# Moving two pairs of squares and a table preload to a later place in ScalarE's order

## The chip, the cores and the metric

The kernel runs on all 8 cores of one Trainium2 chip. Each core works on its own two of the sixteen sequences with no exchange between cores, and the metric is the device time in microseconds of the slowest core. A core has a matrix engine (TensorE, PE in the profile), a vector engine (VectorE, DVE), an engine for activation functions (ScalarE, ACT), GpSimd (POOL) and SyncE (SP). Each runs its own instruction stream in order, and semaphores order the streams against each other. Of POOL and SP only the DMA queues matter here: SP loads x, POOL stores the result.

## The reference

It is one adaLN layer over x of 16 sequences x 4096 tokens x 1024 channels, in float32. The modulation rows come from a small product; then there are two residual branches.

```python
mod = (silu(c) @ wmod).reshape(16, 6, 1, 1024)
sa, ca, ga, sb, cb, gb = mod[:, 0], ..., mod[:, 5]
h = layernorm(x) * (1 + ca) + sa
h = h @ w_in.T + b_in
state = sigmoid(a) * state + b * h_t        # scan over the 4096 tokens' order
x = x + ga * (ys @ w_out.T + b_out)
h = layernorm(x) * (1 + cb) + sb
x = x + gb * tanh(h @ weight @ aux_weight1 @ aux_weight2 + bias)
```

The attention stand-in is a linear input projection, a first-order scan along time, and a linear output projection. The feed-forward branch is three linear maps in a row, which the kernel multiplies together once into a single matrix Wc, and a tanh.

## The kernel before, in words

A setup part builds the combined matrix, the modulation vectors and the broadcast rows (about the first 475 us). The main part then walks over 8192 tokens per core in 32 chunks of 256 tokens (two blocks `tb` of 128). Every float32 matrix product is made as three bf16 products of high and low halves, which DVE splits off (`v_split`).

The main part is one loop over 33 periods, `k` = 0 to 32, on every engine. A period holds the scan branch of chunk k, the second half (LN2, feed-forward) of chunk k-1, and the first layer norm (LN1) of chunk k+1. The order of each stream is written out by hand in `stream_T` (TensorE), `stream_V` (VectorE) and `stream_SC` (ScalarE):

- TensorE: MM1(k), 8 groups i = 0 to 7 of 24 matmuls (`t_MM1`, L702), each group into PSUM bank 2 + i % 2; then the transposes TR2(k-1) and TR1(k+1) (L682); then MM3(k-1) (L750) and MM2(k) (L725). Group i of MM1 waits until ScalarE has taken group i-2 out of its bank (`prev23`).
- ScalarE: evU(k, i) copies group i of MM1 out of PSUM with scale and bias into `su` (L808). SQ(k+1, 1) and SQ(k-1, 2) (`sc_SQ`, L766) are two Square instructions each, over 128x1024, whose accumulated sums are the second moments for LN1 and LN2; they write the squares themselves into `sLNxm1`, which is scratch then. SQRT (L778) makes the standard deviation out of the variance that DVE returns. evA and ev2 (L785, L795) take out the transposes, TANH (L818) ends the feed-forward branch.
- VectorE: v_epiA (residual of branch one, L636 to L646), scans of groups 0 and 1 (`v_scan`, L619), v_LN2 (L578 to L599), scans 2 and 3, v_LN1 (L547 to L568), scans 4 to 7, three splits, and v_epiF (L659 to L671).

Both layer norms bounce between the two engines. DVE reduces x to a sum (L578 in LN2), waits for ScalarE's squares ("sq2"), computes the variance (L582 to L588, "vv2"); ScalarE takes the root ("sqrt2"); DVE goes on with the reciprocal and normalises. The tanh and the square root need different activation tables, so each period changes the table twice. L913 is a Sqrt on one column into a dummy tile, `s_dum`: it has the table for Sqrt loaded ahead of the first real SQRT. In period 32 there is no chunk k, so no evU; in periods 31 and 32 there is no SQ(k+1, 1).

SP loads chunk k+1 of x into one of three buffers `sx` once the store of chunk k-2 is out ("xload", "store").

Of the kernel before, what the change touches and what calls it, by code (L numbers as in the profile page):

```python
# [9 lines left out]
AF = mybir.ActivationFunctionType  # L10
# [8 lines left out]
NCH = TC // CH  # L19
# [5 lines left out]
def build_program(tc=TC, debug=False):  # L25
    EMIT_LOG.clear()
    NCH = tc // CH
# [24 lines left out]
    with contextlib.ExitStack() as stp:  # L52
        def sb(name, shape, dt=F32):
            return stp.enter_context(nc.sbuf_tensor(name, shape, dt))
# [17 lines left out]
        s_A = sb("s_A", [128, KB])  # L72
# [406 lines left out]
        s_dum = sb("s_dum", [128, 1])  # L479
# [40 lines left out]
        E = EV()  # L520
# [239 lines left out]
        def sc_SQ(E, sc, k, which):  # L760
            xap = lambda tb: sx[:, k % 3, tb, :]
            acc = s_s2a if which == 1 else s_s2b
            for tb in range(TB):
                if tb:
                    E.op(lambda: sc.drain())
                f = (lambda tb=tb: sc.activation(  # L766
                    sLNxm1[:, 0:4, :], xap(tb), AF.Square,
                    accum_out=acc[:, tb:tb + 1]))
                if tb < TB - 1:
                    E.op(f)  # L770
                else:
                    E.inc(s_sq, f, ("sq1" if which == 1 else "sq2", k))

        def sc_SQRT(E, sc, k, which):
            vin = s_vara if which == 1 else s_varb
            vout = s_sda if which == 1 else s_sdb
            E.wait(("vv1" if which == 1 else "vv2", k))
            E.inc(s_sq, lambda: sc.activation(vout[:], vin[:], AF.Sqrt),  # L778
                  ("sqrt1" if which == 1 else "sqrt2", k))

        def sc_evA(E, sc, k):
            bi = k // NBCH
            for j in range(KB):
                E.wait(("tr1", k, j))
                E.inc(s_b01, lambda j=j, bi=bi: sc.activation(  # L785
                    sLNxm1[:, j, :], pb[j % 2][:, 0:CH], AF.Identity,
                    scale=s_ca1[:, bi * 8 + j:bi * 8 + j + 1],
                    bias=s_sa[:, bi * 8 + j:bi * 8 + j + 1]),
                    ("evA", k, j))

        def sc_ev2(E, sc, k):
            bi = k // NBCH
            for j in range(KB):
                E.wait(("tr2", k, j))
                E.inc(s_b01, lambda j=j, bi=bi: sc.activation(  # L795
                    sLNxm2[:, j, :], pb[j % 2][:, 0:CH], AF.Identity,
                    scale=s_cb1[:, bi * 8 + j:bi * 8 + j + 1],
                    bias=s_sb[:, bi * 8 + j:bi * 8 + j + 1]),
                    ("ev2", k, j))

        def sc_evU(E, sc, k, i0=0, i1=KB):
            for i in range(i0, i1):
                E.wait(("mm1", k, i))
                if i >= 2:
                    E.wait(("scan", k, i - 2))
                elif k >= 1:
                    E.wait(("scan", k - 1, i + 6))
                E.inc(s_b23, lambda i=i: sc.activation(  # L808
                    su[:, i % 2, :], pb[2 + (i % 2)][:, 0:CH], AF.Identity,
                    scale=s_bv[:, i:i + 1], bias=s_bbi[:, i:i + 1]),  # L810
                    ("evU", k, i))

        def sc_TANH(E, sc, k):
            for tb in range(TB):
                E.wait(("epiFp", k, tb))
                if tb:
                    E.op(lambda: sc.drain())
                E.inc(s_th, lambda tb=tb: sc.activation(  # L818
                    sy_flat[:, tb * D:(tb + 1) * D],
                    sy_flat[:, tb * D:(tb + 1) * D], AF.Tanh),  # L820
                      ("tanh", k, tb))
# [78 lines left out]
        def stream_SC(E, sc):  # L900
            E.eng, E.engname = sc, "scalar"
            E.wait(("xload", 0))
            sc_SQ(E, sc, 0, 1)
            sc_SQRT(E, sc, 0, 1)
            sc_evA(E, sc, 0)
            for k in range(NPER):
                if k + 1 < NCH:
                    E.wait(("xload", k + 1))
                    E.wait(("vv1", k))
                    E.wait(("spA", k))  # L910
                    sc_SQ(E, sc, k + 1, 1)
                E.op(lambda: sc.drain())
                E.op(lambda: sc.activation(s_dum[:], s_A[:, 0:1], AF.Sqrt))  # L913
                if k < NCH:
                    sc_evU(E, sc, k, 0, 2)
                if 0 <= k - 1:
                    E.wait(("x2", k - 1))
                    E.wait(("vv2", k - 2) if k >= 2 else None)
                    sc_SQ(E, sc, k - 1, 2)
                if 0 <= k - 1:  # L920
                    sc_SQRT(E, sc, k - 1, 2)
                if k < NCH:
                    sc_evU(E, sc, k, 2, 4)
                if k + 1 < NCH:
                    sc_SQRT(E, sc, k + 1, 1)
                if k < NCH:
                    sc_evU(E, sc, k, 4, KB)
                if 0 <= k - 1:
                    if k < NCH:
                        E.wait(("spA", k))  # L930
                    sc_ev2(E, sc, k - 1)
                if k + 1 < NCH:
                    sc_evA(E, sc, k + 1)
                if 0 <= k - 1:
                    sc_TANH(E, sc, k - 1)
# [4 lines left out]
        stream_T(E, None)  # L940
        stream_V(E, None)
        stream_SC(E, None)

        E.plan = False
        EMIT_LOG.append(("__BLOCK__", "bar", "", 0))
        with nc.Block() as blk:
            @blk.sync
            def _(sy):
                stream_sync(E, sy)

            @blk.gpsimd
            def _(gp):
                stream_gp(E, gp)

            @blk.tensor
            def _(te):
                stream_T(E, te)

            @blk.vector
            def _(ve):  # L960
                stream_V(E, ve)

            @blk.scalar
            def _(sc):
                stream_SC(E, sc)
# [68 lines left out]
```

How the kernel before makes its waits and increments, by code:

```python
        def W(eng, engname, smp, val):  # L110
            EMIT_LOG.append((engname, "w", NAME[id(smp)], val))
            if val > 0:
                eng.wait_ge(smp, val)
# [1 line left out]
        def I(ins, engname, smp, val=1):  # L115
            EMIT_LOG.append((engname, "i", NAME[id(smp)], val))
            return ins.then_inc(smp, val)
# [383 lines left out]
            def inc(self, sem, f, key=None, by=1):  # L501
                nm = NAME[id(sem)]
                if self.plan:
                    v = self.counts.get(nm, 0) + by
                    self.counts[nm] = v
                    if key is not None:
                        assert key not in self.events, key
                        self.events[key] = (sem, v)
                else:
                    EMIT_LOG.append((self.engname, "i", nm, by))
                    f().then_inc(sem, by)
# [1 line left out]
            def wait(self, key):  # L513
                if key is None or self.plan:
                    return
                sem, v = self.events[key]
                EMIT_LOG.append((self.engname, "w", NAME[id(sem)], v))
                self.eng.wait_ge(sem, v)
```

## Time and profile before

| | |
|---|---|
| median of 12 runs | 2985.88 us (2972.57 to 3238.04) |
| the profiled execution's own time | 2979.61 us |
| its span on the slowest core | 2977.9 us |
| spans of the 8 cores | 2957.1 to 2977.9 us |
| busy in the span | PE 86%, DVE 49%, ACT 24%, POOL 1% |
| mean granted TensorE clock | 0.927 of full speed |

The span runs from the first to the last instruction of the slowest core; the execution's own time is 1.7 us longer. In the timelines below, a row gives the start in us, the duration in us, the engine, the line, the operation, what is written and read, how many instructions are merged into the row, and in brackets the idle time of the engine just before it, with what ended that idle time. A PE row's end is modelled, and consecutive PE rows overlap.

### The profile page before, as it was taken

The page shows a single profiled execution, that of the slowest core. Times are in us where ns is not written, and L with a number is a line of the kernel's source. Part 1 is how long each engine was busy: PE and PEld are TensorE (multiplying, and loading weights), DVE is VectorE, ACT ScalarE, POOL GpSimd, SP SyncE. Part 2 cuts the span into 40 slices and gives each one's busy share as a digit, 9 for nine tenths or more (in the row PEclk, how much of TensorE's full clock was granted, in tenths as well). Part 3 has the DMA queues.
Part 4 walks back from the last instruction along what each step waited for, and adds up shares of the span by engine and source line. Part 5 has one row for each costly group of instructions (what it writes and reads, how often), then busy time and mean ns, then how long its engine had stood idle before and what let it go on. Part 6 is the DMA issues. An engine that isn't in the chain of part 4 may idle for free.

```text
span 2977.9 us, 36603 instructions; the slowest of 8 cores (2957.1 to 2977.9 us)
## 1 busy us (share of the span) xinstructions
PE 2567.3 (86%) x14157; PEld 1435.1 (48%) x14300; DVE 1460.8 (49%) x2038; ACT 719.9 (24%) x1253; POOL 35.0 (1%) x58
## 2 busy tenths in 40 slices
PE   0979633899999999999999999999999999999995
PEld 0432112555555555555555555555555555555552
DVE  3232224555555555555555555555555555555543
ACT  0000001323332222222222222222323223233321
POOL 0000000000000000000000000000000000000000
PEclk9999856999999999999999999999999999999997
DMA  4013441000000000000000010000000000000000
GB/s 135 36 57 132 152 135 43 1 29 29 29 29 29 29 29 29 29 29 29 29 29 29 29 50 29 29 29 29 29 29 29 29 28 19 25 21 23 29 15 29
DMA packets 49254, 118.99 MB, mean 40 GB/s; under 512 B 14352, under 2 KB 14481, under 8 KB 49084
## 3 DMA queue, kind: packets, MB, share of 16 engines
q1 hardware_dynamic: 37996, 75.67, 7.8%
q0 software_dynamic: 11088, 40.97, 3.6%
q8 instruction: 116, 1.90, 0.3%
q14 instruction: 54, 0.44, 0.1%
HBM read 81.44 MB, written 35.20 MB: 39 GB/s over the span
## 4 chain that ended last, share of the span: by engine, by line
PE 58%; DVE 11%; ACT 6%; issue 4%; DVEq 3%; DMA 0%; ACTq 0%; POOL 0%; POOLq 0%
PE pb L750 23%; PE pb L725 22%; PE pb L702 8%; PE pb L682 6%; DVE sy_t L619 3%; ACT sLNxm L795 2%; DVE s_s1a L547 2%; ACT su L808 2%; ACT sLNxm L785 1%; DVE sx L642 1%; DVE stmp L636 1%; DVE s_s1b L578 1%; DVE sx L646 1%; DVEq L580 1%; DVEq L549 1%
## 5 line engine op out<-in xcount | busy, mean ns | idle before, releaser
L659 DVE TENSOR_TENSOR sy_t<-pb,s_BIASC 128x512 f32<-128x512 f32 x128 | 82.5, 686 | 494.4 <-PE pb L750 494.4
L702 PE MATMUL pb<-shi,s_winT_hi 128*128 128x256 bf16 x2048 | 266.0, 273 | 62.7 <-ACT su L808 58.2
L750 PE MATMUL pb<-s_Wc_hi,shi 128*128 128x512 bf16 x960 | 267.8, 421 | 18.4 <-DVE slo L610 10.1
L702 PE MATMUL pb<-slo,s_winT_hi 128*128 128x256 bf16 x2048 | 266.0, 273 | 0.0
L702 PE MATMUL pb<-shi,s_winT_lo 128*128 128x256 bf16 x2048 | 265.4, 273 | 0.0
L636 DVE TENSOR_TENSOR stmp<-pb,s_GA 128x512 f32<-128x512 f32 x128 | 88.6, 692 | 338.7 <-PE pb L725 322.6
L702 PEld LDWEIGHTS pb<-shi,s_winT_hi 128*128 128x128 bf16 x2048 | 196.2, 98 | 107.6 <-issue 78.7
L750 PE MATMUL pb<-s_Wc_lo,shi 128*128 128x512 bf16 x1024 | 246.3, 384 | 0.0
L682 PE MATMUL pb<-s_id,sLNxB 128*128 128x128 f32 x512 | 148.0, 402 | 113.9 <-DVE sLNxB L568 79.7
L619 DVE TENSOR_TENSOR_SCAN sy_t<-s_A,scarry,su 128x256 f32<-128x256 f32 x256 | 185.1, 744 | 124.3 <-ACT su L808 119.3
L725 PE MATMUL pb<-s_woutT_hi,shiY 128*128 128x512 bf16 x960 | 239.9, 381 | 4.9 <-DVE sloY L610 1.6
L766 ACT ACTIVATE sLNxm<-sx 128x1024 f32<-128x1024 f32 x128 | 134.9, 1054 | 447.8 <-DMA sx<-x 414.6
L725 PE MATMUL pb<-s_woutT_lo,shiY 128*128 128x512 bf16 x1024 | 242.4, 380 | 0.0
L725 PE MATMUL pb<-s_woutT_hi,sloY 128*128 128x512 bf16 x1024 | 241.9, 379 | 0.0
L750 PE MATMUL pb<-s_Wc_hi,slo 128*128 128x512 bf16 x1024 | 241.9, 379 | 0.0
L808 ACT ACTIVATE su<-pb,s_bbi,s_bv 128x256 f32<-128x256 f32 x256 | 138.8, 563 | 342.4 <-PE pb L702 205.4
L702 PEld LDWEIGHTS pb<-slo,s_winT_hi 128*128 128x128 bf16 x2048 | 200.8, 98 | 23.5
L702 PEld LDWEIGHTS pb<-shi,s_winT_lo 128*128 128x128 bf16 x2048 | 200.4, 98 | 23.2
L750 PEld LDWEIGHTS pb<-s_Wc_hi,shi 128*128 128x128 bf16 x1024 | 111.3, 109 | 151.1 <-issue 55.6
L750 PEld LDWEIGHTS pb<-s_Wc_lo,shi 128*128 128x128 bf16 x1024 | 102.1, 100 | 128.1 <-issue 13.1
L682 PEld LDWEIGHTS pb<-s_id,sLNxB 128*128 128x128 f32 x512 | 69.0, 189 | 190.2 <-issue 190.2
L725 PEld LDWEIGHTS pb<-s_woutT_hi,shiY 128*128 128x128 bf16 x1024 | 100.4, 98 | 123.1 <-issue 3.2
(108 smaller groups left out, 2489.0 us busy)
## 6 DMA issues: line engine op xcount, KB each, us to landing
sx<-x SPq DMA_DIRECT2D x32, 1024.0 KB, 4.9
out<-sx POOLq DMA_DIRECT2D x32, 1024.0 KB, 4.4
B<-wmod SPq DMA_DIRECT2D x12, 2048.0 KB, 9.2
B<-a SPq DMA_DIRECT2D x2, 4096.0 KB, 17.3
B<-wT SPq DMA_DIRECT2D x1, 4096.0 KB, 16.6
B<-winT SPq DMA_DIRECT2D x1, 4096.0 KB
B4b<-woutT POOLq DMA_DIRECT2D x1, 4096.0 KB, 29.9
gascr<-s_GA POOLq DMA_DIRECT2D x1, 512.0 KB, 3.0
```

Source lines behind the costliest of these rows:

```text
L547: E.op(lambda tb=tb: ve.reduce_sum(s_s1a[:, tb:tb + 1], sx[:, k % 3, tb, :], axis=AX.X))
L549: E.op(lambda: ve.drain())
L619: E.inc(s_scan, lambda i=i: ve.tensor_tensor_scan(sy_t[:, i, :], s_A[:, i:i + 1].broadcast_to([128, CH]), su[:, i % 2, :], scarry[:, i:i + ...
L636: E.inc(s_b47, lambda tb=tb, n=n: ve.tensor_tensor(stmp[:], pb[4 + 2 * tb + n][:], s_GA[:, n * 512:(n + 1) * 512], ALU.mult), ("epiAp", k, ...
L659: E.inc(s_b47, lambda tb=tb, n=n: ve.tensor_tensor(sy_flat[:, tb * D + n * 512:tb * D + (n + 1) * 512], pb[4 + 2 * tb + n][:], s_BIASC[:, ...
L682: f = (lambda j=j, tb=tb, buf=buf: te.transpose(pb[j % 2][:, tb * 128:(tb + 1) * 128], buf[:, tb, j * 128:(j + 1) * 128], s_id[:]))
L702: st=(m == 1), sp=(m == nmm): te.matmul(p[:, 0:CH], wt[:, kk, i * 128:(i + 1) * 128], at[:, kk, :], start=st, stop=sp))
L725: te.matmul(p[:], yt[:, kk, tb * 128:(tb + 1) * 128], wt[:, kk, n * 512:(n + 1) * 512], start=st, stop=sp))
L750: te.matmul(p[:], at[:, kk, tb * 128:(tb + 1) * 128], wt[:, kk, n * 512:(n + 1) * 512], start=st, stop=sp))
L766: f = (lambda tb=tb: sc.activation(sLNxm1[:, 0:4, :], xap(tb), AF.Square, accum_out=acc[:, tb:tb + 1]))
L795: E.inc(s_b01, lambda j=j, bi=bi: sc.activation(sLNxm2[:, j, :], pb[j % 2][:, 0:CH], AF.Identity, scale=s_cb1[:, bi * 8 + j:bi * 8 + j + 1 ...
L808: E.inc(s_b23, lambda i=i: sc.activation(su[:, i % 2, :], pb[2 + (i % 2)][:, 0:CH], AF.Identity, scale=s_bv[:, i:i + 1], bias=s_bbi[:, i:i ...
```

## The change

In `stream_SC`, the order of ScalarE's work in a period changes. Before: SQ(k+1, 1), the dummy Sqrt, evU groups 0 and 1, SQ(k-1, 2), SQRT(k-1, 2), evU groups 2 and 3, and so on. After: evU groups 0 and 1, SQ(k+1, 1), SQ(k-1, 2), the dummy Sqrt, SQRT(k-1, 2), evU groups 2 and 3, and so on. Each pair of squares keeps its semaphore waits. A `drain`, which waits until ScalarE's own earlier writes are done, now stands between the two pairs, which write the same scratch tile. No instruction that computes is added or removed.

```diff
@@ stream_SC
             for k in range(NPER):
+                if k < NCH:
+                    sc_evU(E, sc, k, 0, 2)
                 if k + 1 < NCH:
                     E.wait(("xload", k + 1))
                     E.wait(("vv1", k))
                     E.wait(("spA", k))
                     sc_SQ(E, sc, k + 1, 1)
-                E.op(lambda: sc.drain())
-                E.op(lambda: sc.activation(s_dum[:], s_A[:, 0:1], AF.Sqrt))
-                if k < NCH:
-                    sc_evU(E, sc, k, 0, 2)
                 if 0 <= k - 1:
                     E.wait(("x2", k - 1))
                     E.wait(("vv2", k - 2) if k >= 2 else None)
+                    E.op(lambda: sc.drain())
                     sc_SQ(E, sc, k - 1, 2)
+                E.op(lambda: sc.drain())
+                E.op(lambda: sc.activation(s_dum[:], s_A[:, 0:1], AF.Sqrt))
                 if 0 <= k - 1:
                     sc_SQRT(E, sc, k - 1, 2)
                 if k < NCH:
```

## Rows read from the trace of the kernel before

**Rows 1.** The page: busy time by engine, and the chain that ended last by engine

```profile
PE 2567.3 (86%) x14157; PEld 1435.1 (48%) x14300; DVE 1460.8 (49%) x2038; ACT 719.9 (24%) x1253; POOL 35.0 (1%) x58
...
PE 58%; DVE 11%; ACT 6%; issue 4%; DVEq 3%; DMA 0%; ACTq 0%; POOL 0%; POOLq 0%
```

**Rows 2.** Waits over the span: total us, times, longest us

```profile
PE pb L702 <- ACT su L808: 58.2, 62, 1.8
ACT s_sdb L778 <- DVE s_varb L588: 57.2, 32, 2.1
```

**Rows 3.** Timeline of PE in one MM1: groups 0, 2, 4 and 6

```profile
1621.94 1.04 PE L702 MATMUL pb<-shi,s_winT_hi 128*128 128x256 bf16 x8
...
1627.18 1.04 PE L702 MATMUL pb<-shi,s_winT_hi 128*128 128x256 bf16 x8
...
1632.95 1.03 PE L702 MATMUL pb<-shi,s_winT_hi 128*128 128x256 bf16 x8 [0.37 <-ACT su L808]
...
1639.83 1.03 PE L702 MATMUL pb<-shi,s_winT_hi 128*128 128x256 bf16 x8 [1.48 <-ACT su L808]
```

**Rows 4.** Timeline of ACT in the same period

```profile
1618.63 1.06 ACT L766 ACTIVATE sLNxm<-sx 128x1024 f32<-128x1024 f32 x1 [14.65 <-DMA sx<-x]
...
1621.06 1.28 ACT L913 ACT_TABLE_LOAD   x1
1622.35 0.20 ACT L913 ACTIVATE s_dum<-s_A 128x1 f32<-128x1 f32 x1
1624.88 0.56 ACT L808 ACTIVATE su<-pb,s_bbi,s_bv 128x256 f32<-128x256 f32 x1 [2.32 <-PE pb L702]
1627.50 0.56 ACT L808 ACTIVATE su<-pb,s_bbi,s_bv 128x256 f32<-128x256 f32 x1 [2.06 <-DVE sy_t L619]
1627.96 1.04 ACT L766 ACTIVATE sLNxm<-sx 128x1024 f32<-128x1024 f32 x1
...
1632.10 0.20 ACT L778 ACTIVATE s_sdb<-s_varb 128x2 f32<-128x2 f32 x1 [1.79 <-DVE s_varb L588]
1632.24 1.06 ACT L808 ACTIVATE su<-pb,s_bbi,s_bv 128x256 f32<-128x256 f32 x2
...
1639.12 1.02 ACT L808 ACTIVATE su<-pb,s_bbi,s_bv 128x256 f32<-128x256 f32 x2
```

**Rows 5.** Timeline of DVE in the same period

```profile
1625.31 1.23 DVE L646 TENSOR_TENSOR sx<-sx,s_GAB 128x1024 f32<-128x1024 f32 x1
...
1628.83 2.32 DVE L578 TENSOR_REDUCE s_s1b<-sx 128x1 f32<-128x1024 f32 x2
1631.30 0.17 DVE L582 TENSOR_SCALAR s_nmb<-s_s1b 128x2 f32<-128x2 f32 x1
```

**Rows 6.** Timeline of ACT in other periods: 1, 17, 31 and 32

```profile
563.37 0.20 ACT L778 ACTIVATE s_sdb<-s_varb 128x2 f32<-128x2 f32 x1 [1.79 <-DVE s_varb L588]
...
1773.02 1.06 ACT L766 ACTIVATE sLNxm<-sx 128x1024 f32<-128x1024 f32 x1 [17.52 <-DMA sx<-x]
...
2855.07 0.20 ACT L778 ACTIVATE s_sdb<-s_varb 128x2 f32<-128x2 f32 x1 [1.79 <-DVE s_varb L588]
...
2923.93 1.06 ACT L766 ACTIVATE sLNxm<-sx 128x1024 f32<-128x1024 f32 x1 [21.15 <-DVE sx L646]
...
2927.21 0.20 ACT L778 ACTIVATE s_sdb<-s_varb 128x2 f32<-128x2 f32 x1 [0.91 <-DVE s_varb L588]
```

**Rows 7.** Groups by line, ACT: busy us, mean ns, idle before

```profile
L913 ACT ACT_TABLE_LOAD x31 | 39.8, 1283 | 2.3 <-issue 0.3
...
L913 ACT ACTIVATE s_dum<-s_A 128x1 f32<-128x1 f32 x33 | 6.7, 203 | 0.5
```

**Rows 8.** Busy time and granted clock (PEclk): two whole periods, and 1626 to 1646 us

```profile
1022.08:1097.34 75.26, 69.76 (x415) 41.16 (x417) 41.16 (x60) 22.07 (x39) 0.70 (x1) 0.98 0.08 29
...
1172.62:1250.05 77.43, 72.60 (x415) 42.00 (x417) 41.17 (x60) 22.59 (x39) 0.70 (x1) 0.93 0.08 28
...
1626.00:1646.00 20.00, 17.82 (x161) 15.37 (x158) 14.71 (x28) 6.29 (x14) 0.00 (x0) 1.00 0.01 1
```

## The prediction

> **What bounds the kernel now.** I read the page first: TensorE is busy for 86% of the span and makes up most of the chain that ended last, while ScalarE is busy for 24% [rows 1]. So what counts is where TensorE stands still, and whether ScalarE's new order makes it stand longer. Next I read the waits. TensorE lost 58.2 us in 62 waits of MM1 (L702) for an evU copy (L808) [rows 2], some two for a period. The timelines of one period show which two. MM1's groups come 2.62 us apart (5.24 for two, 1621.94 to 1627.18) [rows 3]. Group 2, which needs evU 0, starts at 1627.18 without a stall, and group 4 stalls for 0.37 us and group 6 for 1.48 us [rows 3]. Group 4 needs evU 2, and ScalarE gives evU 2 only after SQRT of LN2 (1632.10, then 1632.24) [rows 4]. Group 6 needs evU 4, which stands behind the SQRT of LN1 and came out at 1639.12 [rows 4].
>
> So inside MM1 the end is set by a chain through LN2: DVE's residual ends (L646, 1626.54), two scans and the sum reduction (L578, to 1631.15), variance (L582 on), SQRT at 1632.10, evU 2, TensorE's group 4; and on DVE normalising, scans 2 and 3 and LN1, SQRT of LN1, evU 4, group 6 [rows 3 to 5]. Whatever delays the SQRT of LN2 delays group 4, all of LN1 behind it on DVE, and then group 6, by the same amount. TR2, TR1, MM3 and MM2 are queued behind group 7, so the period grows by it.
>
> **What the change takes off that chain: nothing.** It puts evU 0 and evU 1 ahead of SQ(k+1, 1) and the dummy. Before, ScalarE had been idle for 2.32 us when evU 0 came at 1624.88, 2.9 us after the start of MM1, and the wait was for TensorE's group 0 itself [rows 4]. evU 1 was 2.62 later, the spacing of the groups. Neither can come earlier.
>
> **What it adds.** SQ(k+1, 1) and the dummy with its table load ran from 1618.63 to 1622.55 [rows 4], beside MM2 and the first group of MM1, while ScalarE had nothing else to do. That cover is gone; they now stand between evU 1 and the SQRT of LN2, with DVE and TensorE waiting behind.
>
> Count from the first Square behind evU 1, at 1627.96, to the SQRT of LN2. Now it is 4.14 us (1632.10), of which ScalarE idles 1.79 for DVE's variance [rows 4]. Over all periods that idle time is 57.2 us in 32 waits [rows 2]; without period 32's 0.91 [rows 6] it is 56.3 in 31, 1.82 each, so the mean count is 4.17 us.
>
> After the change there are these terms:
> - the pair for LN1: 2.43 us (1618.63 to 1621.06, from its first Square to the instruction behind it) [rows 4];
> - the pair for LN2 in front of the dummy: 2.43 again;
> - the table load up to the dummy: 1.29 (1621.06 to 1622.35) [rows 4];
> - from the dummy to the next small instruction: 0.14, as from SQRT to evU 2 (1632.10 to 1632.24) [rows 4].
>
> The sum is 6.29 us. The other condition of SQRT is DVE's variance. Period 32 shows how long that takes when DVE's reduction does not come last: 3.28 us from the first Square to SQRT (2923.93 to 2927.21) [rows 6]. With the LN1 pair ahead that is 2.43 + 3.28 = 5.71. ScalarE's own 6.29 is later and decides, by 0.58. The drain between the pairs I take as free: the two Squares of a pair already have one between them, inside the 2.43.
>
> So the SQRT of LN2 moves by 6.29 - 4.17 = 2.12 us. Group 4 had no slack to give (it stalled already), so its stall grows from 0.37 to about 2.5 and the period by 2.12.
>
> How often: 31 loads stand ahead of the dummy, though it runs 33 times [rows 7]; periods 0 and 1 have none, since no tanh has run yet. By period:
> - periods 2 to 30 pay in full: 29 x 2.12 = 61.5 us;
> - period 1 has no load, so DVE's 5.71 decides: 5.71 less 4.15 (it too has 1.79 idle [rows 6]), 1.6 us;
> - period 31 has no LN1 pair; load and dummy (1.43) fit into its 1.79 of idle time [rows 6]: nothing;
> - period 32 has no evU, and load and dummy come behind the squares: 2.43 + 1.29 + 0.14 = 3.86 instead of 3.28, 0.6 us;
> - period 0 has no LN2; evU 2 comes at most 0.5 late, and group 4 wants it one group (2.62) later: nothing.
>
> Together 63.7 us. The wait of SQ(k+1, 1) for x moves too, and costs nothing: x is there by 1618.63 and is now wanted 9.3 us later [rows 4]. LN1's variance wants that pair only after LN2's normalising, so that it comes later is free too.
>
> The profiled execution took 2979.61 us, 6.3 less than the median of the twelve runs. Added: 2979.6 + 63.7 = 3043, and I say 3044.
>
> **What the trace of before does not show: TensorE's clock in a stall of 2.5 us.** It falls now during the transposes. A period at a mean of 0.98 took 75.26 us and one at 0.93 took 77.43; the mean of 30 periods is 76.39 (563.37 to 2855.07) [rows 6, 8]. In the stretch with both of today's stalls the clock stayed at 1.00, that is 2.4 GHz [rows 8]. If the stretch is shifted so that every period falls into the quicker or the slower kind, 29 periods give -33 or +30 us. If the longer stall itself brings a fall to 1.2 GHz, I price it like the difference of these two periods, 2.17 us. Groups 4 and 5 would run slowly then, and most of that is taken back, since group 6 stands for 1.48 us anyway: 0.7 us net, 20 us over 29 periods; with nothing taken back, 63. The low bound is 0, and I take it, because today's stalls cost no clock.
>
> The Trainium skill, "TensorE: Matmul & The Clock Gate", section "HAM oscillation — how this bites in real kernels", says that idle gaps between bursts of matmuls can put the array back to half clock, each time anew. No run here shows a gap of 2.5 us inside MM1. By that rule the sum would be the clock rival's below.
>
> **Rivals.**
> 1. *The clock falls in the longer stall.* Today's 1.48 us leaves it at full speed, which speaks against; the transposes with gaps, where it does fall, speak for. Time: 3043 + 20 to 63, 3063 to 3106. Chance 0.12.
> 2. *The table is changed elsewhere.* If the copy of evU is not in the table that tanh leaves behind, the change to another table would come ahead of evU 0 and the dummy's load might vanish. ScalarE would be free for it: evU 0 would end about 1.3 late, at 1626.7, before group 2 at 1627.18 [rows 3, 4]. Then DVE's 5.71 decides everywhere: 30 x 1.54, 46 us, 3026. Today Square follows tanh without a load (1618.63, no load ahead [rows 4]), but no copy does. Chance 0.07. The Trainium skill, "ScalarE: Activation LUTs", section "Table sets: the hidden batching unit", says that cheap functions such as copy and identity are in every set; by that this rival is out.
> 3. *A load costs more where something waits for it.* The same page, section "What ACT_TABLE_LOAD costs", counts 1.28 us and a drain of 1.38 for every switch, 2.66 in all. By that the sum would be 29 x 1.38 = 40 larger. The row agrees with the 1.28 but not with the drain: the dummy starts 1.29 after the load [rows 4]. As a mechanism of this kernel, the work in flight at the load would have to be waited for; a Square's end lies right ahead of the load today too. Time 3083. Chance 0.03.
> 4. *It ends faster or equal: x is late.* Where x comes late, SQ(k+1, 1) holds up evU 0 today, and TensorE's group 2; the new order sets evU 0 free. The pair, load, dummy and copy take 2.43 + 1.29 + 0.14 + 0.56 = 4.4 us, and group 2 starts 5.24 after group 0. So it decides where x lands over 0.8 us after MM1 starts, and makes up for the loss only from 2.9 us on. In the period shown x was there 3.3 before; the latest, 1773.02 [rows 6], still left it at some two waits a period, which are those of groups 4 and 6 [rows 2]. With x at 5 us after MM1's start in every period of the timed runs, the old order would lose 4.2 us there and the new one its 2.1: 63 us under the kernel before, 2917. Chance 0.05, of which 0.03 within 0.3%, where x lands near the 2.9.
>
> **How the numbers follow.** My forecast has 0.73, with a range of its own of 3030 to 3058 for the phase of the clock. Rivals 2 and, in its lower half, 1 are taken in: 3022 to 3074. Left out are the far half of rival 1, rivals 3 and 4 and the far ends of the clock's phase, some 0.18. About 0.3%, 9 us, is what a measurement of this kernel can tell from no change; all cases but rival 4 lie over it. Slower 0.95, same 0.03, faster 0.02.
>
> **What would show it.** Right: evU 0 and 1 stand as now against MM1's start; the LN1 pair starts 0.46 us after evU 1; the load comes directly ahead of the SQRT of LN2, which waits for nothing; the stall ahead of group 4 is about 2.5 us and that of group 6 stays near 1.5; PE's waits in L702 for L808 rise from 58 to about 120 us. Wrong: a load ahead of evU 0 (rival 2), a granted clock under 1.00 in groups 4 to 7 (rival 1), an idle stretch between load and dummy (rival 3), or group 4's stall unchanged, which would say that the chain through LN2 was not the one that sets the end.

## The result, and the profile after

The changed kernel takes 1.0222 times as long as the kernel before, with a 95% interval of [1.0199, 1.0244]: on a median of 2978.98 us beside it, some 66 us more (59 to 73). Its profiled execution took 3044.45 us, 64.8 more than that of before; the forecast was 3044. The median of its twelve runs is 3064.63 us (3043.13 to 3255.03), because in some of them the cores of one die ran at a lower granted clock; those are left out of the ratio and of everything below. Of the two pairs of squares in the title only the one for LN1 passes evU 0 and 1; the pair for LN2 stood behind them already, and now has the LN1 pair ahead of it.

The page, with the busy times and the chain that ended last, to be held against [rows 1]:

```profile
PE 2585.2 (85%) x14300; PEld 1436.5 (47%) x14300; DVE 1460.5 (48%) x2038; ACT 712.7 (23%) x1253; POOL 34.9 (1%) x58
...
PE 59%; DVE 9%; ACT 8%; issue 4%; ACTq 3%; DVEq 2%; DMA 0%; POOL 0%; POOLq 0%
```

No engine has more to do (the 143 matmuls that TensorE seems to have gained are records missing from the trace of before; ScalarE has the same 1253 instructions). What grew is ScalarE's part in the chain, from 6 to 8%, and that of its queue, at the cost of DVE's. The waits of the changed kernel (total us, times, longest us) say where:

```profile
PE pb L702 <- ACT su L808: 118.9, 61, 2.7
...
DVE s_nmb L582 <- ACT sLNxm L766: 51.6, 31, 1.7
```

MM1's waits for an evU copy rose from 58.2 to 118.9 us [rows 2]. SQRT of LN2's wait for the variance, 57.2 us in [rows 2], is gone: instead DVE now waits 51.6 us for the squares. The groups by line (busy, mean ns, idle before) complete it:

```profile
L920 ACT ACT_TABLE_LOAD x31 | 39.8, 1283 | 2.0
...
L778 ACT ACTIVATE s_sdb<-s_varb 128x2 f32<-128x2 f32 x32 | 6.0, 188 | 0.7 <-DVE s_varb L588 0.6
```

There are still 31 loads of the same 1283 ns [rows 7], and the SQRT of LN2 now waits 0.6 us for DVE in the whole run. One period in the timeline of ACT, to be held against [rows 4]:

```profile
1573.99 0.57 ACT L808 ACTIVATE su<-pb,s_bbi,s_bv 128x256 f32<-128x256 f32 x1 [20.52 <-PE pb L702]
1576.61 0.57 ACT L808 ACTIVATE su<-pb,s_bbi,s_bv 128x256 f32<-128x256 f32 x1 [2.05 <-DVE sy_t L619]
1577.08 1.05 ACT L766 ACTIVATE sLNxm<-sx 128x1024 f32<-128x1024 f32 x1
...
1579.51 1.06 ACT L766 ACTIVATE sLNxm<-sx 128x1024 f32<-128x1024 f32 x1
...
1581.94 1.28 ACT L920 ACT_TABLE_LOAD   x1
1583.23 0.20 ACT L920 ACTIVATE s_dum<-s_A 128x1 f32<-128x1 f32 x1
1583.34 0.19 ACT L778 ACTIVATE s_sdb<-s_varb 128x2 f32<-128x2 f32 x1
1583.44 1.00 ACT L808 ACTIVATE su<-pb,s_bbi,s_bv 128x256 f32<-128x256 f32 x2
```

From the first Square to the SQRT it is 2.43 + 2.43 + 1.29 + 0.11 = 6.26 us, without an idle stretch; before it was 4.14. And TensorE's groups 0, 2, 4 and 6 of that MM1, to be held against [rows 3]:

```profile
1571.06 1.04 PE L702 MATMUL pb<-shi,s_winT_hi 128*128 128x256 bf16 x8
...
1576.30 1.04 PE L702 MATMUL pb<-shi,s_winT_hi 128*128 128x256 bf16 x8
...
1584.13 1.03 PE L702 MATMUL pb<-shi,s_winT_hi 128*128 128x256 bf16 x8 [2.43 <-ACT su L808]
...
1591.06 1.03 PE L702 MATMUL pb<-shi,s_winT_hi 128*128 128x256 bf16 x8 [1.53 <-ACT su L808]
```

Group 2 comes 5.24 after group 0 as before. Group 4 stalls for 2.43 instead of 0.37, group 6 for 1.53 instead of 1.48: 2.11 us more in MM1.

Last, 27 periods in a row, from the SQRT of LN2 in period 2 to that in period 29, in windows of busy time and granted clock. Before:

```profile
651.32:2713.69 2062.37, 1924.11 (x11126) 1124.69 (x11233) 1111.54 (x1622) 605.04 (x1053) 20.75 (x30) 0.95 0.08 29
```

and after:

```profile
653.10:2776.18 2123.08, 1939.73 (x11234) 1125.64 (x11233) 1111.35 (x1622) 598.70 (x1053) 20.68 (x30) 0.95 0.08 28
```

A period took 2062.37 / 27 = 76.38 us and takes 2123.08 / 27 = 78.63, 2.25 more at the same mean clock of 0.95.

### The profile page after: what moved, and what is told of

Its sections match the earlier page's. It is cut to its first block, busy times and chain, and to the rows that moved or that the text cites. A ratio compares the mean times of both kernels' runs of the same rounds, so it can differ in the third digit from the quotient of the medians.

```text
span 3042.9 us, 36778 instructions; the slowest of 8 cores (3027.1 to 3042.9 us)
## 1 busy us (share of the span) xinstructions
PE 2585.2 (85%) x14300; PEld 1436.5 (47%) x14300; DVE 1460.5 (48%) x2038; ACT 712.7 (23%) x1253; POOL 34.9 (1%) x58
## 4 chain that ended last, share of the span: by engine, by line
PE 59%; DVE 9%; ACT 8%; issue 4%; ACTq 3%; DVEq 2%; DMA 0%; POOL 0%; POOLq 0%
PE pb L750 23%; PE pb L725 22%; PE pb L702 7%; PE pb L682 6%; ACT sLNxm L766 2%; ACT sLNxm L795 2%; DVE s_s1a L547 2%; DVE sy_t L619 2%; ACT su L808 2%; ACTq L765 1%; DVE sx L642 1%; DVE stmp L636 1%; DVE sx L646 1%; DVEq L549 1%; ACTq L917 1%
## 5 line engine op out<-in xcount | busy, mean ns | idle before, releaser
L702 PE MATMUL pb<-shi,s_winT_hi 128*128 128x256 bf16 x2048 | 266.9, 273 | 123.4 <-ACT su L808 118.9
L808 ACT ACTIVATE su<-pb,s_bbi,s_bv 128x256 f32<-128x256 f32 x256 | 137.5, 561 | 885.4 <-PE pb L702 753.5
L750 PE MATMUL pb<-s_Wc_hi,shi 128*128 128x512 bf16 x1024 | 293.5, 439 | 9.4 <-DVE slo L610 9.4
L702 PEld LDWEIGHTS pb<-shi,s_winT_hi 128*128 128x128 bf16 x2048 | 196.8, 98 | 168.8 <-issue 139.1
L702 PE MATMUL pb<-shi,s_winT_lo 128*128 128x256 bf16 x2048 | 268.0, 274 | 0.0
L702 PE MATMUL pb<-slo,s_winT_hi 128*128 128x256 bf16 x2048 | 267.6, 274 | 0.0
L702 PEld LDWEIGHTS pb<-shi,s_winT_lo 128*128 128x128 bf16 x2048 | 201.7, 98 | 24.4
L702 PEld LDWEIGHTS pb<-slo,s_winT_hi 128*128 128x128 bf16 x2048 | 201.3, 98 | 24.0
L750 PEld LDWEIGHTS pb<-s_Wc_hi,slo 128*128 128x128 bf16 x1024 | 100.2, 98 | 120.8
L725 PEld LDWEIGHTS pb<-s_woutT_lo,shiY 128*128 128x128 bf16 x1024 | 100.2, 98 | 120.8
```

Of the source, the lines that this page charges most:

```text
L702: st=(m == 1), sp=(m == nmm): te.matmul(p[:, 0:CH], wt[:, kk, i * 128:(i + 1) * 128], at[:, kk, :], start=st, stop=sp))
L725: te.matmul(p[:], yt[:, kk, tb * 128:(tb + 1) * 128], wt[:, kk, n * 512:(n + 1) * 512], start=st, stop=sp))
L750: te.matmul(p[:], at[:, kk, tb * 128:(tb + 1) * 128], wt[:, kk, n * 512:(n + 1) * 512], start=st, stop=sp))
L808: E.inc(s_b23, lambda i=i: sc.activation(su[:, i % 2, :], pb[2 + (i % 2)][:, 0:CH], AF.Identity, scale=s_bv[:, i:i + 1], bias=s_bbi[:, i:i ...
```

## The experiments

Two numbers are read in each: what MM1's stalls changed by in one period, and what the period changed by. All edits are against the kernel before unless it is said otherwise. The letters in the expectations are theories. A is that of the prediction: the time goes with the count from evU 1 to the SQRT of LN2, under the two conditions ScalarE and DVE. B: the table load is dear wherever something waits behind it. C: ScalarE's added work counts, whatever covers it. D: what matters is where evU 0 and 1 stand. E: DVE's chain is the bound. F, formed after the first runs: the stretches that TensorE runs at its lower clock give way, so that a period keeps one length under small changes.

### Only the dummy moved

```diff
                     sc_SQ(E, sc, k + 1, 1)
-                E.op(lambda: sc.drain())
-                E.op(lambda: sc.activation(s_dum[:], s_A[:, 0:1], AF.Sqrt))
                 if k < NCH:
                     sc_evU(E, sc, k, 0, 2)
...
+                    E.op(lambda: sc.drain())
                     sc_SQ(E, sc, k - 1, 2)
+                E.op(lambda: sc.drain())
+                E.op(lambda: sc.activation(s_dum[:], s_A[:, 0:1], AF.Sqrt))
```

> Order of ScalarE as before the change, except that only the dummy Sqrt with its table load moves behind the pair of squares for LN2. Theory A (what counts is the time from the first square behind evU 1 to the SQRT of LN2; DVE's variance sets it at 4.17 us today): 2.43 + 1.29 + 0.14 = 3.86 us, less than 4.17, so the load is hidden in idle time: within 0.3% of the kernel before (about +1 us, from period 32). Rival B (a table load costs where it stands close to the Sqrt that needs it, or lies on the path whole): 29 x 1.4 us, about +41 us, 1.4% slower.

Ratio 0.9988 [0.9963, 1.0013], profiled 2974.81 us. Its timeline of ACT:

```profile
1623.50 1.06 ACT L766 ACTIVATE sLNxm<-sx 128x1024 f32<-128x1024 f32 x1
...
1625.93 1.28 ACT L920 ACT_TABLE_LOAD   x1
...
1627.46 0.20 ACT L778 ACTIVATE s_sdb<-s_varb 128x2 f32<-128x2 f32 x1
```

The count is 3.96 us, and MM1's waits are 58.2 us as before. (The drain that this edit puts in front of the LN2 pair lets its first Square start 0.65 us after evU 1, where it was 0.46; counted from evU 1, the SQRT comes at 4.61 us for 4.60.) The very load that stands in front of the SQRT in the changed kernel costs nothing here: it fills what was the SQRT's idle wait of 1.79 [rows 4]. B falls, and with it rival 3.

### Only the LN1 pair moved

```diff
             for k in range(NPER):
+                E.op(lambda: sc.drain())
+                E.op(lambda: sc.activation(s_dum[:], s_A[:, 0:1], AF.Sqrt))
+                if k < NCH:
+                    sc_evU(E, sc, k, 0, 2)
                 ...
                     sc_SQ(E, sc, k + 1, 1)
-                E.op(lambda: sc.drain())
-                E.op(lambda: sc.activation(s_dum[:], s_A[:, 0:1], AF.Sqrt))
-                if k < NCH:
-                    sc_evU(E, sc, k, 0, 2)
                 ...
+                    E.op(lambda: sc.drain())
                     sc_SQ(E, sc, k - 1, 2)
```

> Only the pair of squares for LN1 moves behind evU 0 and 1; the dummy with its table load stands first in the period, beside TensorE's MM2. Theory A: 2.43 + 3.28 = 5.71 us through DVE's variance instead of 4.17, 1.54 us in each of 30 periods: +46 us, about 3026. Rival B (the load is most of the loss, the squares are hidden): within 0.3% of before. Rival C (all of ScalarE's moved work counts, without the 1.8 us that were idle): 2.43 x 30, +73 us.

Ratio 1.0207 [1.0136, 1.0278], profiled 3040.91 us, 61 more than the kernel before where A gave 46. The timelines of ACT and of PE show A's terms nevertheless:

```profile
1655.54 1.05 ACT L766 ACTIVATE sLNxm<-sx 128x1024 f32<-128x1024 f32 x1
...
1661.26 0.20 ACT L778 ACTIVATE s_sdb<-s_varb 128x2 f32<-128x2 f32 x1 [0.91 <-DVE s_varb L588]
```

```profile
1662.11 1.03 PE L702 MATMUL pb<-shi,s_winT_hi 128*128 128x256 bf16 x8 [1.95 <-ACT su L808]
...
1668.99 1.03 PE L702 MATMUL pb<-shi,s_winT_hi 128*128 128x256 bf16 x8 [1.48 <-ACT su L808]
```

The count is 5.72 us, DVE's condition to 0.01, and the SQRT waits for DVE. MM1's waits are 105.6 us, 47 more than before: the 46 of A. But 27 periods took this:

```profile
652.37:2772.38 2120.01, 1933.94 (x11126) 1133.57 (x11233) 1111.68 (x1622) 597.92 (x1053) 20.75 (x30) 0.94 0.08 28
```

That is 78.52 a period, 2.14 more than before, of which MM1's stalls explain 1.58. The other 0.56 comes with a lower mean clock, 0.94 for 0.95 (0.916 to 0.919 over the whole span on the eight cores, where the changed kernel has 0.929 to 0.932). The chain explains the stalls, not the whole time; that is why F was formed. (By stage, in the table further down, the 0.56 lies in the transposes and MM3.)

### The load and dummy between the two pairs

```diff
             for k in range(NPER):
+                if k < NCH:
+                    sc_evU(E, sc, k, 0, 2)
                 ...
                     sc_SQ(E, sc, k + 1, 1)
                 E.op(lambda: sc.drain())
                 E.op(lambda: sc.activation(s_dum[:], s_A[:, 0:1], AF.Sqrt))
-                if k < NCH:
-                    sc_evU(E, sc, k, 0, 2)
                 ...
+                    E.op(lambda: sc.drain())
                     sc_SQ(E, sc, k - 1, 2)
```

> The same instructions behind evU 1 as in the changed kernel, but the dummy with its load stands between the two pairs of squares and not behind them. Theory A: DVE's variance now waits for the load too: 2.43 + 1.43 + 3.28 = 7.14 us instead of 4.17, 2.97 us in 29 periods and 1.7 in period 1: about +88 us, 3067. Rival C (the sum of ScalarE's work between evU 1 and the SQRT counts, whatever its order): as the changed kernel, about +65 us.

Ratio 1.0277 [1.0213, 1.0341], profiled 3049.68 us. In the timelines of ACT and PE:

```profile
1660.10 1.05 ACT L766 ACTIVATE sLNxm<-sx 128x1024 f32<-128x1024 f32 x1
...
1667.36 0.20 ACT L778 ACTIVATE s_sdb<-s_varb 128x2 f32<-128x2 f32 x1 [0.91 <-DVE s_varb L588]
```

```profile
1668.21 1.03 PE L702 MATMUL pb<-shi,s_winT_hi 128*128 128x256 bf16 x8 [3.49 <-ACT su L808]
1669.08 1.57 PE L702 MATMUL pb<-slo,s_winT_hi 128*128 128x256 bf16 x8
1670.45 1.91 PE L702 MATMUL pb<-shi,s_winT_lo 128*128 128x256 bf16 x8
...
1675.11 1.04 PE L702 MATMUL pb<-shi,s_winT_hi 128*128 128x256 bf16 x8
```

The count is 7.26 where A has 7.14, and with the same work on ScalarE as in the changed kernel group 4 stalls 1.06 longer: the order alone decides, so C falls as a sum of work. Behind this stall the matmuls run at the lower of TensorE's two levels, 1.2 instead of 2.4 GHz (eight take 1.9 us instead of 1.04; the mean granted clock is 0.61 from 1669.08 to 1673.50), which is what rival 1 feared. It costs nothing inside MM1: group 6 no longer stalls, and starts 6.90 us after group 4, as it did before (6.88 in [rows 3]), because its date is set by DVE's way to the SQRT of LN1. The waits of L702 fall to 36 for that reason. MM1 is longer by 3.19 us a period than before (mean of 27), but the period (78.91) by 2.53 only.

### The LN1 pair behind evU 3

```diff
             for k in range(NPER):
-                if k + 1 < NCH:
-                    E.wait(("xload", k + 1))
-                    E.wait(("vv1", k))
-                    E.wait(("spA", k))
-                    sc_SQ(E, sc, k + 1, 1)
-                E.op(lambda: sc.drain())
-                E.op(lambda: sc.activation(s_dum[:], s_A[:, 0:1], AF.Sqrt))
                 if k < NCH:
                     sc_evU(E, sc, k, 0, 2)
...
+                    E.op(lambda: sc.drain())
                     sc_SQ(E, sc, k - 1, 2)
+                E.op(lambda: sc.drain())
+                E.op(lambda: sc.activation(s_dum[:], s_A[:, 0:1], AF.Sqrt))
...
                     sc_evU(E, sc, k, 2, 4)
                 if k + 1 < NCH:
+                    E.wait(("xload", k + 1))
+                    E.wait(("vv1", k))
+                    E.wait(("spA", k))
+                    E.op(lambda: sc.drain())
+                    sc_SQ(E, sc, k + 1, 1)
                     sc_SQRT(E, sc, k + 1, 1)
```

> As the changed kernel, evU 0 and 1 first and the dummy behind the squares for LN2, but the pair of squares for LN1 stands behind evU 3, where ScalarE idles 5.7 us for DVE's variance of LN1. Theory A: 3.86 us to the SQRT of LN2, hidden, and the pair is done some 2 us before DVE asks for it: within 0.3% of the kernel before, +1 us. Rival D (the loss comes from the new place of evU 0 and 1, or from the clock of TensorE, not from what stands ahead of the SQRT): as the changed kernel, +65 us.

Ratio 1.0001 [0.9975, 1.0026], profiled 2976.89 us. Its ACT behind the SQRT of LN2:

```profile
1629.32 0.20 ACT L778 ACTIVATE s_sdb<-s_varb 128x2 f32<-128x2 f32 x1
...
1630.60 1.06 ACT L766 ACTIVATE sLNxm<-sx 128x1024 f32<-128x1024 f32 x1
...
1636.19 0.20 ACT L778 ACTIVATE s_sda<-s_vara 128x2 f32<-128x2 f32 x1 [3.23 <-DVE s_vara L557]
```

evU 0 and 1 come first and the load stands in front of the SQRT, as in the changed kernel; only the LN1 pair stands in an idle stretch of some 5.7 us (2.43 + 3.23), of which 3.23 are still left. The loss is gone, so D falls, and the pair in front of the LN2 pair is what turns a hidden load into a loss.

### One and two useless Squares in front of SQRT of LN2

The diff is that of one; with two, the range is 2.

```diff
                     sc_SQ(E, sc, k - 1, 2)
                 if 0 <= k - 1:
+                    for _ in range(1):
+                        E.op(lambda: sc.drain())
+                        E.op(lambda: sc.activation(
+                            sLNxm1[:, 0:4, :], sx[:, (k - 1) % 3, 0, :],
+                            AF.Square, accum_out=s_dum[:]))
```

> Order of the kernel before with one useless square of 1.22 us more behind the pair for LN2, ahead of the SQRT of LN2. Theory A: 2.43 + 1.22 + 0.14 = 3.8 us, less than 4.17, hidden in the idle time of 1.82: within 0.3% of before. Rival C (every piece of ScalarE's work on this stretch counts in full): 31 x 1.22, +38 us, 1.3% slower.

> As the one before with two useless squares. Theory A: 2.43 + 2.43 + 0.14 = 5.0 us instead of 4.17, 0.84 us in each of 31 periods and in period 32 1.7: about +28 us, 0.9% slower. Rival C: 32 x 2.43, +78 us. If TensorE's clock makes a step of its own as the stall grows, the time lies off 28 by up to 20.

One: ratio 1.0012 [0.9974, 1.005], profiled 2974.83; its SQRT still waits 0.56 for DVE. Two: 1.0048 [1.003, 1.0066], profiled 2990.42, half of what was expected. The timelines of ACT and PE with two show why:

```profile
1632.57 1.04 ACT L766 ACTIVATE sLNxm<-sx 128x1024 f32<-128x1024 f32 x1
...
1637.28 0.19 ACT L778 ACTIVATE s_sdb<-s_varb 128x2 f32<-128x2 f32 x1
```

```profile
1638.06 1.03 PE L702 MATMUL pb<-shi,s_winT_hi 128*128 128x256 bf16 x8 [0.87 <-ACT su L808]
```

The count is 4.71, not the 5.0 that I had expected: the SQRT follows the last Square sooner than a further Square does. So the stall grows by 0.50, MM1's waits from 58.2 to 73.8 (+16), and the time by about 14. One Square of 1.22 fits into the idle 1.79 and two of them don't: the point at which the cover ends is where A puts it.

### Copies that wait on nothing put ahead of the two SQRTs

```diff
                     sc_SQ(E, sc, k - 1, 2)
+                if k < NCH:
+                    sc_evU(E, sc, k, 2, 3)
                 if 0 <= k - 1:
                     sc_SQRT(E, sc, k - 1, 2)
                 if k < NCH:
-                    sc_evU(E, sc, k, 2, 4)
+                    sc_evU(E, sc, k, 3, 6)
                 if k + 1 < NCH:
                     sc_SQRT(E, sc, k + 1, 1)
                 if k < NCH:
-                    sc_evU(E, sc, k, 4, KB)
+                    sc_evU(E, sc, k, 6, KB)
```

> Order of the kernel before, except that evU 2 stands ahead of the SQRT of LN2, and evU 4 and 5 ahead of the SQRT of LN1. Theory A (both stalls of MM1 come from evU standing behind a SQRT that waits for DVE): evU 2 can come at 1630.1 and evU 4 at about 1635.3 in the period shown, so neither group 4 nor group 6 waits. 0.37 + 1.48 = 1.9 us less in each of some 30 periods: -55 us, about 2923, 1.9% faster. Rival E (DVE's chain of scans and layer norms sets the period, and TensorE's stalls only show it): the time comes back at the transposes, within 0.3% of before.

Ratio 0.9854 [0.9818, 0.989], profiled 2935.56 us: faster than both kernels, by 44 us in the profile where 55 were expected. Its ACT:

```profile
1608.11 1.05 ACT L766 ACTIVATE sLNxm<-sx 128x1024 f32<-128x1024 f32 x1
...
1610.37 0.55 ACT L808 ACTIVATE su<-pb,s_bbi,s_bv 128x256 f32<-128x256 f32 x1
1612.25 0.20 ACT L778 ACTIVATE s_sdb<-s_varb 128x2 f32<-128x2 f32 x1 [1.33 <-DVE s_varb L588]
1612.88 0.56 ACT L808 ACTIVATE su<-pb,s_bbi,s_bv 128x256 f32<-128x256 f32 x1 [0.43 <-PE pb L702]
```

evU 2 fills part of the SQRT's idle wait, and the wait of PE's L702 for L808 is gone from its list of waits. The SQRT itself is hardly later (4.14 behind the first Square, as before). So the 58 us of stalls came from two waiting instructions standing in front of copies that didn't wait for them, and E falls: the time follows, though DVE's chain to the SQRT is as long as before. But not all of it comes back: MM1 is 2.24 us shorter a period (20.96 for 23.20, mean of 27; the bracketed idle times, 0.37 and 1.48, understate it), and the period only 1.44.

### Useless TensorE work: does the clock give it back?

In MM2 of each period, 4, 2 or 8 matmuls of 128x512 whose result is overwritten. At the full clock eight such matmuls follow one another in 1.73 us, 0.216 each. The diff is that of four:

```diff
                     p = pb[4 + 2 * tb + n]
+                    if tb == 0 and n == 0:
+                        for _ in range(4):
+                            E.op(lambda p=p: te.matmul(
+                                p[:], shiY[:, 0, 0:128], s_woutT_hi[:, 0, 0:512],
+                                start=True, stop=True))
```

Four in the changed kernel, in the one with early copies, and in the kernel before:

> The changed kernel with four useless matmuls of 128x512 more at the head of MM2 in every period: by the spacing of MM2's own (1.73 us for 8), 0.86 us of TensorE's dense work. Theory A (the period is a plain sum of TensorE's work and its stalls): 32 x 0.86, +28 us over the changed kernel, about 3072. Theory F (in the changed kernel every period comes out at 78.5 us because the stretch at the lower clock in the transposes grows or shrinks until it does; the periods of the squares-late kernel are the same 78.5 although its chain is 0.2 us shorter): the period stays at 78.5, the mean granted clock of a period rises, and the time stays within 0.3% of the changed kernel, about 3044.

> The kernel with evU 2, 4 and 5 early and the same four matmuls more. Its periods come out at 75.0 us now with more of the lower clock than before (mean 0.915 against 0.929). Theory A: +28 us over that kernel, about 2960. Theory F: the period stays at 75.0 and the granted clock rises: about 2932, within 0.3% of that kernel.

> The kernel before with the same four matmuls more. Its periods change between 74.1 and 77.6 us, so nothing holds them at one length. Theory A: +28 us, about 3004, 0.9% slower. Theory F: also about +28 us, at most 10 less or more, since the mean over its kinds of periods moves with the work; the period would be 77.2 on average.

Two in the changed kernel, and eight in the one with early copies:

> The changed kernel with two useless matmuls in a period instead of four, 0.43 us of TensorE's work. Theory A: 32 x 0.43, +14 us over the changed kernel, about 3058. Theory F (the stretch at the lower clock gives way until the period is 78.5 us again): within 0.3% of the changed kernel, 3044 to 3048, with periods of 78.5.

> The kernel with evU 2, 4 and 5 early and eight useless matmuls in a period, 1.73 us of TensorE's work. With four, the period stayed at 74.8 and the mean clock rose from 0.915 to 0.932. Theory A: 32 x 1.73, +55 us over the kernel without them, about 2987. Theory F has an end where the lower clock is used up: from 0.932 a rise to about 0.95 is left (a period spent 6.3 us of 75 there with four), which is worth some 0.9 us, so the period goes to 75.1 or at most 75.8: 2935 to 2960.

All kernels side by side. MM1, the transposes with MM3, and MM2 are the stages of a period on the profiled core, each from its first matmul to the first of the next stage, in us and as the mean of 27 periods; the mean period is from SQRT to SQRT as above. (The transposes and MM3 stand together, since in some traces records of MM3's first matmuls are missing.)

| kernel | MM1 | transposes and MM3 | MM2 | mean period | against before | ratio |
|---|---|---|---|---|---|---|
| before | 23.20 | 32.46 | 20.72 | 76.38 | 0 | 1 |
| two useless Squares | 23.71 | 32.34 | 20.72 | 76.78 | +0.40 | 1.0048 |
| LN1 pair alone | 24.78 | 33.01 | 20.72 | 78.52 | +2.14 | 1.0207 |
| changed | 25.36 | 32.55 | 20.72 | 78.63 | +2.25 | 1.0222 |
| dummy between | 26.39 | 31.81 | 20.72 | 78.91 | +2.53 | 1.0277 |
| early copies | 20.96 | 33.25 | 20.72 | 74.95 | -1.44 | 0.9854 |
| before, 4 matmuls | 23.19 | 32.73 | 21.58 | 77.52 | +1.14 | 1.0116 [1.0095, 1.0138] |
| changed, 2 matmuls | 25.30 | 32.10 | 21.15 | 78.55 | +2.17 | 1.0218 [1.0201, 1.0234] |
| changed, 4 matmuls | 25.31 | 31.91 | 21.58 | 78.81 | +2.42 | 1.032 [1.0231, 1.0409] |
| early copies, 4 matmuls | 20.96 | 32.30 | 21.58 | 74.86 | -1.52 | 0.9902 [0.9869, 0.9935] |
| early copies, 8 matmuls | 20.96 | 32.07 | 22.45 | 75.48 | -0.90 | 0.9928 [0.9903, 0.9953] |

In the kernel before, four matmuls are paid in full and more. In the changed kernel two cost nothing and four 0.18 of their 0.86. With early copies four cost nothing and eight 0.53 of 1.73. The mean spans of the eight cores in the profiled executions agree: with four, 3001.7 us for 2967.1 in the kernel before, 3042.9 for 3035.2 in the changed one and 2922.4 for 2925.0 with early copies, and with eight 2940.2. The ratios of the timed runs, whose intervals are wide there, would have some 29 us of the 27.6 for four in the changed kernel and 14 with early copies, and 22 of the 55 for eight; so for the four the profiled executions alone show what is taken up; for the two and the eight the ratios do as well.

F holds in so far as added work on the bounding engine is partly or wholly taken up, but not as a rule that a period keeps its length: in the kernel before nothing is taken up, and of the eight matmuls about a third is paid (75.48, inside F's own 75.1 to 75.8). The stages say where it happens. MM2 grows by all that is added (20.72 to 21.15, 21.58 and 22.45) and MM1 keeps its length. What gives way is the stretch of transposes and MM3; in the kernel before that stretch grows. With early copies the clock was higher with the four; the windows of 27 periods, without

```profile
648.88:2672.39 2023.51, 1952.26 (x11232) 1137.44 (x11232) 1111.35 (x1622) 612.55 (x1055) 20.68 (x30) 0.93 0.08 30
```

and with them:

```profile
646.95:2668.15 2021.20, 1931.66 (x11232) 1136.25 (x11340) 1111.62 (x1622) 607.74 (x1055) 20.68 (x30) 0.96 0.08 30
```

With two in the changed kernel the clock was lower, and the period was still no longer:

```profile
657.15:2777.99 2120.84, 1978.86 (x11288) 1150.18 (x11287) 1111.13 (x1622) 601.47 (x1053) 20.69 (x30) 0.94 0.08 28
```

MM1's waits fell to

```profile
PE pb L702 <- ACT su L813: 77.1, 36, 2.7
```

without MM1 getting shorter: the lower clock lay in groups 4 and 5 there, in most periods, where group 6's stall absorbs it. It lay less in MM3 in turn. This is one MM3 of the changed kernel, and one with two matmuls added, as windows of busy time and granted clock (0.93 and 0.95):

```profile
1606.48:1628.84 22.36, 22.36 (x97) 9.79 (x96) 7.16 (x6) 3.07 (x4) 0.00 (x0) 0.93 0.00 1
...
1611.66:1633.36 21.70, 21.70 (x98) 9.67 (x96) 6.97 (x5) 3.05 (x4) 0.00 (x0) 0.95 0.00 1
```

A period, in the mean of 27 and of the eight cores, has 0.46 us of MM1 and 3.07 us of MM3 at the lower clock in the changed kernel, and 3.22 and 1.94 with the two matmuls. So that is where the room for 0.43 us came from. Why the lower clock moved is not shown.

## Why the prediction was right

**The chain and its place.** Right. The load stands directly ahead of the SQRT of LN2, which waits for nothing; group 4's stall is 2.43 (2.5 said), group 6's 1.53 (1.5 said), the waits 118.9 us (120 said). Only the chain is shown by this; that order and not the amount of ScalarE's work decides is shown by the dummy alone (nothing lost) and the dummy between (more lost with the same work).

**Nothing gained from early evU 0 and 1.** Right: with them first and the LN1 pair out of the way the ratio is 1.0001.

**The count of 6.29.** Right: 6.26, with 0.11 for the step from dummy to SQRT where 0.14 was taken. The drain between the pairs costs nothing: the second pair starts 2.43 behind the first.

**DVE's 5.71 as the second condition.** Right, and shown twice: by the LN1 pair alone, and by period 1 of the changed kernel, where the table is there already. In that period's timeline of ACT it is 562.27 - 556.56 = 5.71:

```profile
556.56 1.05 ACT L766 ACTIVATE sLNxm<-sx 128x1024 f32<-128x1024 f32 x1
...
562.27 0.20 ACT L778 ACTIVATE s_sdb<-s_varb 128x2 f32<-128x2 f32 x1 [0.62 <-DVE s_varb L588]
```

**Periods 31 and 32.** Right: 3.95 us from first Square to SQRT in period 31, which is under the 4.14 of before (and its MM1 takes 21.49 us in both kernels), and 3.83 in period 32 (3.86 said):

```profile
2988.52 1.06 ACT L766 ACTIVATE sLNxm<-sx 128x1024 f32<-128x1024 f32 x1 [22.75 <-DVE sx L646]
...
2992.35 0.19 ACT L778 ACTIVATE s_sdb<-s_varb 128x2 f32<-128x2 f32 x1
```

**The clock, taken as zero.** This is the one term that was mis-sized, by little. A period grew by 2.25 on the profiled core, not 2.12, and the mean span of the eight cores by 68.1 us (2967.1 to 3035.2) instead of 63.7. MM1's waits hold 58 of these (116.2 for 58.0, means of the eight cores). Some 4 more are waits of group 6 that the next paragraph tells of, and 0.6 belongs to period 32. The rest, about 5 us, lies outside MM1, in the transposes and MM3: over the eight cores they take 32.50 us a period for 32.35, and MM2 takes 20.72 in both. On the six cores with no record missing in either trace, MM3 is 0.32 longer (22.30 for 21.98) and the transposes 0.16 shorter; over all eight TensorE spends 3.07 us of MM3 at its lower clock instead of 2.43, and 3.76 us of the transposes instead of 4.71. That the term came out small is luck in part: that stretch loses 0.55 us a period with the pair alone and gives back 0.65 with the dummy between. And that 3044 met the profiled 3044.45 so closely is luck: the sum was 63.7, the mean span grew by 68.1, and the profiled time by 64.8. The reason given for zero, that today's stalls cost no clock, said nothing about the rest of the period.

**Rival 1** did happen, in a few periods: on the eight cores 57 to 61 waits are left of 62, and each that is missing is one of group 6, in a period like this one of PE:

```profile
1035.18 1.03 PE L702 MATMUL pb<-shi,s_winT_hi 128*128 128x256 bf16 x8 [2.43 <-ACT su L808]
1036.05 1.62 PE L702 MATMUL pb<-slo,s_winT_hi 128*128 128x256 bf16 x8
1037.47 1.91 PE L702 MATMUL pb<-shi,s_winT_lo 128*128 128x256 bf16 x8
...
1042.11 1.03 PE L702 MATMUL pb<-shi,s_winT_hi 128*128 128x256 bf16 x8
```

Its price was put at 0.7 net; it is nothing, since group 6 starts 6.93 behind group 4 here too. The Trainium skill, "TensorE: Matmul & The Clock Gate", section "HAM oscillation — how this bites in real kernels", has gaps between bursts put the array back to half clock again and again. Its case there is a kernel whose gaps are waits for DMA, longer than the 2.43 us here, so the forecast's "by that rule" went further than the section does. The traces agree where the stall is 3.49 (nearly every period, 26 of 62 waits gone); at 2.43 it is 1 to 5 periods of 30 in the changed kernel, and most of them once two matmuls are added elsewhere in the period, so the gap's length alone does not settle it here.

**Rival 2** is out: no load stands ahead of evU 0, whose copies follow tanh directly, as the Trainium skill's "ScalarE: Activation LUTs", section "Table sets: the hidden batching unit", has it for cheap functions. **Rival 3** is out, by the 1.29 from load to dummy and by the dummy alone. **Rival 4** is out: the idle time ahead of the Squares is put down to DVE's x (22.7 of 29.6 us, period 32) and none of it to a DMA, and the time went the other way:

```profile
L766 ACT ACTIVATE sLNxm<-sx 128x1024 f32<-128x1024 f32 x128 | 134.9, 1054 | 29.6 <-DVE sx L646 22.7
```

## What to carry to other kernels

Price a moved instruction by the idle time at its new place, on the chain that ends last there: the same table load was free in 1.79 us of idle time and part of a 2% loss once 2.43 us of squares stood in front of it. In a stream that runs in order, look for an instruction that waits with others behind it that don't: putting copies ahead of two waiting square roots took all of MM1's stalls and 1.5% of the time. Where one engine's clock is granted in two levels, trust a sum of stalls and work only to about 0.8 us a period in this kernel (the stretch of transposes and MM3 moved by -0.65 to +0.79), and read the period, its stages and the clock beside it.

## What the runs showed that was not expected

Small changes in stalls or work don't pass into the period one to one. With MM1 longer by 1.58, 2.16 and 3.19 us the periods were 78.52, 78.63 and 78.91; with 0.43 us of matmuls added to the second, 78.55. With early copies they were 74.95, and 74.86 with 0.86 us of matmuls more. Only the kernel before paid in full (1.14 for 0.86). The granted clock of these stretches differs (0.93 to 0.96) and with early copies it is higher where there is more work. The stages put all of the difference into the transposes and MM3 (31.81 to 33.25 us), where the lower clock lies as long as it doesn't fall into MM1. Why the lengths gather near 78.5 and 75.0, and what places the stretches of lower clock in the period, these runs don't settle.

The lower clock can also be free of charge: where it fell in groups 4 and 5 of MM1, a stall that stood behind them anyway took it up.
